# Later column sums in the output projection, and fp32 column sums of the residual, in a transformer layer on eight cores

## What is computed

```python
x = x + layernorm(attn(layernorm(x), Wq, Wk, Wv, Wo))       # x: [2, 4096, 2048] fp32
x = x + layernorm(ffn(layernorm(x), gate_w, up_w, down_w, gate_s, up_s, down_s))

def layernorm(x, eps=1e-5):
    m = mean(x); v = var(x)          # over the last axis
    return (x - m) / sqrt(v + eps)

def attn(x, Wq, Wk, Wv, Wo):         # 16 heads of 128, rope, causal
    ...
    return ctx @ Wo.T
```

## Time and profile before

| What | us |
|---|---|
| runs of the kernel before | 4266.18 and 4558.82, median 4412.5 |
| the profiled execution, its own time | 4265.35 |
| its span on core 7, the slowest | 4263.8 |
| spans of the eight cores | 4243.5 to 4263.8 |
| output projection, first matmul to last sum | 2568.5 to 2747.0 |
| x2 sums, first half | 2788.1 to 2812.5 |
| x2 sums, second half | 2883.0 to 2907.1 |

### The profile page before, as it was taken

The page is one execution under the profiler, slowest core; times in us unless marked ns, Lnnn a source line. Parts: engine busy times, 40 slices in busy tenths (PEclk is TensorE's granted clock), DMA queues, the critical chain, the costliest instruction groups (busy, mean ns, idle before and its releaser), DMA issues.

```text
span 4263.8 us, 34533 instructions; the slowest of 8 cores (4243.5 to 4263.8 us)
## 1 busy us (share of the span) xinstructions
PE 3135.4 (74%) x12448; PEld 1159.0 (27%) x12448; DVE 1345.9 (32%) x1249; ACT 738.9 (17%) x780; POOL 404.7 (9%) x287
## 2 busy tenths in 40 slices
PE   5662788898888766878788877624888888788870
PEld 1110233343333322111111112201333333333320
DVE  3674625464554465222222220162000000000012
ACT  2220000000000001444444441122000000000000
POOL 0000000000000000233332330000000000000004
PEclk9775899999999888888888888856999999999985
DMA  5764911101111342111111103122333333343323
GB/s 159 196 177 108 151 55 54 58 35 57 55 55 57 75 78 79 40 40 40 40 33 33 33 3 89 30 79 69 59 59 65 60 63 60 67 80 55 59 37 118
DMA packets 183206, 294.32 MB, mean 69 GB/s; under 512 B 6656, under 2 KB 121344, under 8 KB 180864
## 3 DMA queue, kind: packets, MB, share of 16 engines
q0 software_dynamic: 44352, 102.77, 14.6%
q1 hardware_dynamic: 138688, 189.34, 14.4%
HBM read 323.54 MB, written 71.30 MB: 93 GB/s over the span
## 4 chain that ended last, share of the span: by engine, by line
PE 65%; DVE 13%; DMA 8%; ACT 6%; issue 3%; POOL 2%; another core or an unknown queue 2%; POOLq 0%; ACTq 0%; DVEq 0%; SPq 0%
PE psA L159 23%; PE psB L159 20%; PE psD L159 8%; PE psC L159 7%; PE psE L159 5%; DMA xa<-xctx 2%; ACT esb L547 2%; DMA lns<-ln_scr 2%; POOL esb L557 2%; DVE hdn L737 1%; DVE lno L271 1%; DVE lno L273 1%; ACT gt L734 1%; DVE esb L557 1%
## 5 line engine op out<-in xcount | busy, mean ns | idle before, releaser
L159 PE MATMUL psA<-h,gsb 128*128 128x512 bf16 x1408 | 332.9, 398 | 157.6 <-DVE hdn L737 127.5
L159 PE MATMUL psA<-lns,wk_sb 128*128 128x512 bf16 x1024 | 243.5, 399 | 153.7 <-DMA lns<-ln_scr 92.7
L557 POOL TENSOR_TENSOR esb<-esb,mask_sb 128x1024 bf16<-128x1024 bf16 x128 | 271.1, 2118 | 807.0 <-ACT esb L547 807.0
L159 PE MATMUL psB<-h,usb 128*128 128x512 bf16 x1408 | 311.1, 379 | 0.0
L557 DVE TENSOR_TENSOR esb<-esb,mask_sb 128x1024 bf16<-128x1024 bf16 x128 | 105.7, 826 | 570.4 <-ACT esb L547 570.4
L737 DVE SCALAR_TENSOR_TENSOR hdn<-psB,us_sb,gt 128x1024 bf16<-128x1024 f32 x44 | 56.5, 1284 | 721.7 <-ACT gt L734 721.7
L159 PE MATMUL psD<-wv_sb,lns 128*128 128x512 bf16 x1024 | 236.0, 384 | 12.4 <-DMA wv_sb<-wv 12.4
L159 PE MATMUL psD<-esb,vsb 128*128 128x512 bf16 x512 | 161.2, 398 | 112.3 <-POOL esb L557 79.7
L159 PE MATMUL psE<-esb,ones_c 128*1 128x512 bf16 x768 | 243.7, 400 | 0.0
L159 PE MATMUL psC<-wv_sb,lns 128*128 128x512 bf16 x1024 | 234.0, 382 | 10.4 <-DMA wv_sb<-wv 10.4
L159 PEld LDWEIGHTS psA<-h,gsb 128*128 128x128 bf16 x1408 | 140.0, 101 | 351.7 <-issue 208.2
(11 more groups left out here) (154 smaller groups left out, 3163.1 us busy)
## 6 DMA issues: line engine op xcount, KB each, us to landing
xa<-xctx SPq DMA_DIRECT2D x8, 4096.0 KB, 25.7
gsb<-wg POOLq DMA_DIRECT2D x44, 512.0 KB, 5.2
usb<-wu POOLq DMA_DIRECT2D x44, 512.0 KB, 7.2
dsb<-wd POOLq DMA_DIRECT2D x32, 704.0 KB, 6.3
ln_scr<-lno SPq DMA_DIRECT2D x10, 2048.0 KB, 11.1
lns<-ln_scr SPq DMA_DIRECT2D x8, 2048.0 KB, 11.3
k_scr<-kout SPq DMA_DIRECT2D x128, 128.0 KB, 1.8
v_scr<-vout SPq DMA_DIRECT2D x32, 512.0 KB, 2.7
```

What stands on the lines that cost most here:

```text
L159: en.matmul(o, l, r, start=a, stop=z))
L557: en.tensor_mul(b[:], b[:], m)))
```

## The change

In the output projection the four column sums of block `oc` are moved behind the 32 matmuls of block `oc+1` (a new function `wo_stats`), and those of the last block follow the loop. The evacuation of block `oc` waits for the sums of block `oc-1` as before, which now stand behind its own matmuls.

In the sums of x2 the casts are left out: TensorE sums `x2c` in fp32 with `ones_cf`. The squares are made by ScalarE in two instructions of 8 slices each (128x4096) into one new buffer `x2q8`, and TensorE sums them in bf16 in two groups of eight. For the second group, ScalarE waits until TensorE has read the first.

```diff
+            def wo_stats(j):
+                p.wt("t", sS, evac_done[j])
+                for nt in range(NT):
+                    s1dst = psE[:, 0:512] if nt == 0 else psC[0:1, :]
+                    s2dst = psE[:, 512:1024] if nt == 0 else psD[0:1, :]
+                    add_mm(s1dst, ones_c[:], v4[:, j, nt * 512:(nt + 1) * 512],
+                           j == 0, j == DC - 1)
+                    stat_done[j] = add_mm(s2dst, ones_c[:],
+                                          vsq4[:, nt * 512:(nt + 1) * 512],
+                                          j == 0, j == DC - 1)
...
-                p.wt("s", sT, sT.n)
                 if oc >= 1:
+                    wo_stats(oc - 1)
                     p.wt("s", sT, stat_done[oc - 1])
+                else:
+                    p.wt("s", sT, mm_done[oc])
                 p.dat("s", lambda en, o_=oc, ps_=ps: en.copy(v4[:, o_, :], ps_[:]))
                 evac_done[oc] = p.dat("s", lambda en, ps_=ps: en.activation(
                     vsq4[:], ps_[:], AF.Square))
-                p.wt("t", sS, evac_done[oc])
-                for nt in range(NT):
...
+            wo_stats(DC - 1)
             stats_ready = stat_done[DC - 1]
...
                 p.wt("s", sV, vx2)
-                dc_mm = {}
-                for dc in range(DC):
-                    if dc >= 2:
-                        p.wt("s", sT, dc_mm[dc - 2])
-                    p.dat("s", lambda en, d_=dc, b=x2b_s[dc % 2]: en.copy(b[:], x2c[:, d_, :]))
-                    scp = p.dat("s", lambda en, d_=dc, b=x2sq_s[dc % 2]: en.activation(
-                        b[:], x2c[:, d_, :], AF.Square))
+                for hf in range(2):
+                    if x2q8_busy[0] is not None:
+                        p.wt("s", sT, x2q8_busy[0])
+                    scp = p.dat("s", lambda en, h_=hf: en.activation(
+                        x2q8[:], x2c[:, h_ * 8:(h_ + 1) * 8, :], AF.Square))
+                    if hf == 0:
+                        p.wt("t", sV, vx2)
+                    for dc in range(hf * 8, hf * 8 + 8):
+                        add_mm(psE[:, 0:512], ones_cf[:], x2c[:, dc, :], dc == 0, dc == DC - 1)
                     p.wt("t", sS, scp)
-                    add_mm(psE[:, 0:512], ones_c[:], x2b_s[dc % 2][:], dc == 0, dc == DC - 1)
-                    dc_mm[dc] = add_mm(psE[:, 512:1024], ones_c[:], x2sq_s[dc % 2][:],
-                                       dc == 0, dc == DC - 1)
+                    for dc8 in range(8):
+                        dc = hf * 8 + dc8
+                        x2q8_busy[0] = add_mm(psE[:, 512:1024], ones_c[:], x2q8[:, dc8, :],
+                                              dc == 0, dc == DC - 1)
```

More of the change, by code:

```diff
@@ L616, in build_nc @@
             x2c = pe(nc.sbuf_tensor("x2c", [128, DC, 512], F32))
-            x2b_s = [pe(nc.sbuf_tensor(f"x2b{i}", [128, 512], BF16)) for i in range(2)]
-            x2sq_s = [pe(nc.sbuf_tensor(f"x2sq{i}", [128, 512], BF16)) for i in range(2)]
+            x2q8 = pe(nc.sbuf_tensor("x2q8", [128, 8, 512], BF16))
             evac_done = {}
             stat_done = {}
+            mm_done = {}
+            def wo_stats(j):
[8 more added lines that the diff above has]
+                                          j == 0, j == DC - 1)
             for oc in range(DC):
@@ L632, in build_nc @@
                     for dvc in range(DC):
-                        add_mm(ps[:, nt * 512:(nt + 1) * 512], wos[oc % 2][:, dvc, :],
-                               ctxT[:, dvc, nt * 512:(nt + 1) * 512],
-                               dvc == 0, dvc == DC - 1)
-                p.wt("s", sT, sT.n)
+                        mm_done[oc] = add_mm(ps[:, nt * 512:(nt + 1) * 512],
+                                             wos[oc % 2][:, dvc, :],
+                                             ctxT[:, dvc, nt * 512:(nt + 1) * 512],
+                                             dvc == 0, dvc == DC - 1)
                 if oc >= 1:
+                    wo_stats(oc - 1)
                     p.wt("s", sT, stat_done[oc - 1])
+                else:
+                    p.wt("s", sT, mm_done[oc])
                 p.dat("s", lambda en, o_=oc, ps_=ps: en.copy(v4[:, o_, :], ps_[:]))
@@ L657, in build_nc @@
             x2_store = {}
+            x2q8_busy = [None]
             for nt in range(NT):
```

## The result

| What | us |
|---|---|
| kernel before, median of 15 executions (lowest to highest) | 4454.91 (4262.45 to 4650.43) |
| changed kernel, median of 16 executions (lowest to highest) | 4359.79 (4214.83 to 4573.24) |
| ratio to the kernel before, 95% interval | 0.9906, 0.9872 to 0.9940 |
| profiled execution of the changed kernel, its own time | 4216.06, span 4214.4 |

The medians lie above the profiled executions because in 11 of the 16 executions of the changed kernel (4299.5 us and more) the cores of one die or of both had a lower mean clock, 0.79 to 0.85 against 0.87, and by their times 10 of the 15 of the kernel before were such too; the ratio leaves them out. By the ratio the kernel gained 0.9%, about 40 us, within the 2% that count as no change here. Between the profiled executions the gain is 49.3 us (4265.35 to 4216.06).

A forecast was written before the change was run, and what follows sets the result against it. The prediction took PE's path to bound the kernel, 65% of the last-ending chain of waits. From the profiled 4265.35 us it took 42.9 (projection) and 9.0 (x2 sums), giving 4213 us, range 4197 to 4244.

The forecast's parts named there:

- Which executions the forecast was for: Whole kernel: 4213 us was meant for an execution like the profiled 4265.35 us, with 0.3% of scatter in the range.
- PE's wait for the evacuation goes: Output projection: PE's wait of 2.47 us a block behind ACT's square goes; such waits total 40.8 us.
- The weight load is late next: Output projection: the load of wos ends last at every other block, 16.14 us for two blocks against PE's 15.72.
- Part one: Output projection: column sums of a block moved behind the next block's matmuls gain 42.9 us.
- No blocks at 1.2 GHz once PE hardly rests: Output projection: none of the blocks slowed to 8.71 us by a fallen clock remain, some 3.3 us of the gain.
- Part two: Sums over x2: fp32 sums and large squares take 19.9 us a half, gaining 4.5 a half, 9.0 in all.
- (a): Rival: the clock stays at 1.2 GHz in the x2 sums, losing 20.9 us; time 4243; chance 0.08.
- (b): Rival: projection weight loads bind harder, 7.2 us each, two blocks take 18.0 us; time 4227; chance 0.08.
- (c): Rival: denser matmuls on all eight cores are granted less clock, say 0.865; time 4233; chance 0.05.
- (d): Rival: the projection's stream is held at 1.2 GHz throughout, a block takes 15.5 us; time 4324; chance 0.02.
- (e): Rival: evacuation still ends last, projection blocks stay at 10.5 us and only x2 gains; time 4256; chance 0.03.

The follow-up runs named there:

- early_load: Changed kernel, but the next projection weights are loaded once the matmuls reading the buffer are done, not after the evacuation; ratio 0.9886 to the kernel before.
- both_again: The changed kernel run once more, unaltered, on the chip of the next three runs; ratio 0.9908 to the kernel before, profiled execution 4216.28 us.
- proj_only: Changed kernel with the x2 sums put back as before, so only the later column sums of the projection remain; ratio 0.9922 to the kernel before.
- gate_deferred: Changed kernel, with ScalarE's silu in the gate and up projection started behind the gate matmuls, beside the up matmuls; 4060.97 and 4057.71 us.
- pieces_bf16: Changed kernel, but x2 sums from a bf16 cast, cast and squared in four-slice pieces with two buffers each; 4211.01 us.
- x2_only: Changed kernel with the projection put back as before, so only the fp32 sums of x2 remain; ratio 0.9980 to the kernel before.
- late_load: Changed kernel, but a projection block's weight load waits for the column sums of the block two before; 4322.88 us, ratio 1.0127 to the kernel before.
- all_deferred: Changed kernel plus earlier weight loads, x2 in four chunks, later down-projection column sums and earlier silu in gate and up; 3956.35 us profiled.

## Why the prediction was right or wrong

**Which executions the forecast was for: wrong.** The step that failed is the last of the sum: "the profile agrees with the lower, and the forecast is for an execution like that one". The range of 4197 to 4244 was built around one kind of execution, although one of the two shown, 4558.82, lay outside anything it could hold. The median of 16 is 4359.79, 147 us above the forecast and outside the range, since eleven of them took 4299.5 to 4573.2 us and only five 4214.8 to 4249.2; the median of the kernel before moved as well, from 4412.5 to 4454.91. The 0.3% of scatter had no ground in the two times shown either: even the five differ by 0.8%. Against the profiled execution the forecast of 4213.4 is 2.7 us low, which is partly luck, as the parts below show; its ratio, 4213.4/4265.35 = 0.988, lies within the measured interval.

**PE's wait for the evacuation goes: right.** Only the last block's is left, 2.4 us of 40.8.

**The weight load is late next: right, the pattern less so.** It ends last not at every other block but at eight of 13 on the core shown, and at six to ten on the others. 16.14 us for two blocks were forecast and 16.22 came on the core shown, 16.3 on the mean of the eight. Two terms were off. PE alone needs 15.94 for two blocks, not 15.72 (`early_load`): the 0.1 of a restart falls before the sums as well as behind them (there the sums behind the matmuls of 2608.54 start at 2615.55, after 7.01 us, which are 32 spacings and 0.1). And a load lands in 5.1 us at the median, not 5.3.

**Part one, 42.9 us: right in size, its closeness partly luck.** From the first matmul on, 44.0 in the profiled execution, 43.1 in `both_again`, 42.0 in `proj_only`, each on its slowest core. But the core shown took 134.6 us, the least of the eight; the others took 136.8 to 138.8. Its first block took 8.36 us, where the forecast kept 9.96 and six of the other cores took 9.7 to 10.0. On the mean of the eight cores the stage went from 177.4 to 137.5 us, a gain of 39.9. The forecast had it end in 135.6; block 2 started 10.5 us behind block 1 on the mean, not 9.4, and the later blocks took 8.16, not 8.07.

**No blocks at 1.2 GHz once PE hardly rests: right but for one.** The clock is 0.99 in the stage on the core shown. Before, each core had three such blocks behind the first; in the changed kernel one core of the eight has one, behind a wait for the weights of block 2. `gate_deferred` shows the same for the stage where they had cost more.

**Part two, 9.0 us: right in size, its reason incomplete.** 4.6 and 5.2 us in the two halves. The second was better because the clock rose sooner: its first eight sums took

```profile
2834.99 8.35 PE L159 MATMUL psE<-x2c,ones_cf 128*1 128x512 f32 x16 [29.28 <-DVE x2c L684]
```

against the forecast 9.2. What I did not see is that fp32 is not needed: bf16 in large pieces takes 17.2 us (`pieces_bf16`).

**Rivals.** (a) a low clock in the x2 sums fell by the 0.89 and 0.93 of the changed kernel and by `x2_only`. (b) harder loads fell by the landing of 5.1 us; `late_load` shows what they would have cost. (c) and (d) a lower clock under denser matmuls fell in the profiled executions: 0.99 in the projection, and in `all_deferred` 1.00 over 600 us of nearly unbroken matmuls, on every one of the eight cores. The rule of the Trainium skill (TensorE: Matmul & The Clock Gate, Part 1), by which dense matmuls on three cores of a die bring it to 13/16, does not show in those rows; by it the gain of part one would have been an estimated 20 us, and 44.0 came. What the executions above 4299 us were granted in this stage is not known, so for them (c) stays open. (e) fell by the timeline.

**The 53.8 us of the stages and the 49.3 of the whole.** From the first gate matmul to the end the changed kernel's slowest core takes 4214.4 - 2895.4 = 1319.0 us, that of the kernel before 4263.8 - 2948.5 = 1315.3. Here 3.7 us go again, though the stage's code is the same. That is scatter between cores: in the changed kernel the eight cores take 1313.4 to 1319.3 us, in the kernel before 1314.2 to 1318.8, and the means are the same. Means over the eight cores of each trace, in us:

| Kernel | first projection matmul to last column sum | from there to the first gate matmul | from there to the end |
|---|---|---|---|
| before | 177.4 | 201.7 | 1316.2 |
| changed | 137.5 | 192.2 | 1316.3 |
| `both_again` | 137.4 | 191.9 | 1315.8 |
| `proj_only` | 137.6 | 201.7 | 1314.6 |
| `x2_only` | 177.9 | 192.0 | 1315.1 |
| `early_load` | 133.0 | 192.4 | 1316.3 |

Part one is worth 39.9 us and part two 9.4 (201.7 less 192.2, before rounding), each alone as much as with the other, and no later stage gives anything back.

## What to carry to other kernels

Where PE waits in every block for an evacuation, put the small matmuls that need it behind the next block's large ones, and then follow the waits of every engine to find the load or buffer that was hidden by the old wait. A wait of 3 us can cost PE more than 3 us, since the clock may fall in it; of the 155 us that the same move gained in the stage with the most blocks, 132 were the waits and 23 the clock. Before a stage's gain is put down to a term of the sum, look at all the cores: here the slowest one had the shortest projection of the eight. And state a range for the executions that are counted, not for the one that was profiled.

## What the runs showed of the hardware that was not expected

In the kernel before, the granted clock stayed at 0.50 through 24 us of x2 sums in pairs with a gap of 0.41 us before each, as in the first line. In `pieces_bf16` it rose within eight matmuls nearly in a row, and stayed up though the sums after them left PE waiting for about half of the time: the stretch of 17.2 us, in the second line, has 0.85.

```profile
2791.06 0.58 PE L159 MATMUL psE<-x2b,ones_c 128*1 128x512 bf16 x1 [0.41 <-ACT x2sq L686]
...
2745.80:2763.00 17.20, 9.52 (x32) 2.41 (x32) 0.01 (x1) 15.22 (x8) 0.00 (x0) 0.85 0.65 244
```

In these stages a ScalarE cast from fp32 to bf16 on 128x512 takes 617 ns, on 128x2048 1.90 us and on 128x4096 3.60 us. The last two differ by 0.83 ns an element, so about 0.2 us of each instruction is fixed, and some 0.1 more lies between two. Four slices in one instruction cost ScalarE 2.0 us, not 4 x 0.71 = 2.8.
